# Second expert layer: scatters that add weighted rows to the output in memory, instead of a closing stage of sums

## What is computed

```
x = x + 0.5 * ffn(layernorm(x))          # mixture of experts, weights shared by both ffn calls
x = x + attn(layernorm(x))               # causal convolution, 16 blocks of 128 tokens, 8 heads
x = x + 0.5 * ffn(layernorm(x))

ffn(h):   probs = softmax(h @ router_w.T)        # 8 experts
          vals, idx = top_k(probs, 2); vals = vals / vals.sum(-1)
          out = sum over the two experts e of a token:
                vals_e * (silu(h @ gate_e.T) * (h @ up_e.T)) @ down_e.T      # hidden width 176
```

## Time and profile before

| | |
|---|---|
| median of 3 runs | 756.17 us |
| profiled execution: its own time | 758.16 us |
| profiled execution: span | 756.4 us |
| mean granted TensorE clock | 0.954 of full speed |
| PE busy | 664.9 us, 88% |
| DVE busy | 520.7 us, 69% |
| ACT busy | 491.3 us, 65% |
| POOL busy | 372.7 us, 49% |

### The profile page before, as it was taken

How to read it: one execution, slowest core, us unless ns; L and a number is a source line. 1 busy time by engine, 2 the same in 40 slices (tenths; PEclk the granted TensorE clock), 3 DMA queues, 4 the chain that set the end, 5 groups by cost and what they waited for, 6 DMA issues and landing times. The chain is left out here.

```text
span 756.4 us, 18879 instructions
## 1 busy us (share of the span) xinstructions
PE 664.9 (88%) x5168; PEld 590.6 (78%) x5169; DVE 520.7 (69%) x1829; ACT 491.3 (65%) x1702; POOL 372.7 (49%) x418
## 2 busy tenths in 40 slices
PE   3999799999996699999898989978778999999854
PEld 3986699999993577878787878767557899999743
DVE  6588466666666467787878777858657677777653
ACT  5775566666664278887877868768444566666633
POOL 4200544444424546657787877554545444444500
PEclk9999899999999789999999999999879999999968
DMA  9930345444442211111222221110224543443289
GB/s 307 304 128 10 106 141 151 143 126 133 129 111 83 77 36 36 50 42 52 77 64 64 71 72 60 33 58 22 88 89 122 160 134 120 130 127 125 71 315 351
DMA packets 60424, 85.50 MB, mean 113 GB/s; under 512 B 10032, under 2 KB 46387, under 8 KB 60340
## 3 DMA queue, kind: packets, MB, share of 16 engines
q1 hardware_dynamic: 47332, 49.73, 21.2%
q0 software_dynamic: 13008, 34.69, 14.6%
HBM read 45.77 MB, written 37.44 MB: 110 GB/s over the span
## 5 line engine op out<-in xcount | busy, mean ns | idle before, releaser
L1811 PE MATMUL CC<-w_hi,turned_parts 128*128 x568 | 175.5, 351 | 3.6 <-issue 3.6
L725 POOL DMA_INDIRECT shared<-h_rows,tok_i x71 | 70.2, 988 | 116.4 <-issue 58.9
L1811 PEld LDWEIGHTS CC<-w_hi,turned_parts 128*128 128x128 f32 x568 | 105.4, 193 | 4.4 <-issue 4.3
L742 POOL DMA_INDIRECT y_rows<-shared,y_dest x71 | 70.0, 986 | 76.0 <-DVE y_dest L1349 57.8
L818 ACT ACTIVATE shared<-CC 128x176 f32<-128x176 f32 x142 | 45.2, 319 | 76.1 <-PE CC L1811 70.1
L1811 PE MATMUL CC<-w_lo,turned_parts 128*128 x284 | 93.3, 328 | 0.0
L934 ACT ACTIVATE pr<-SS,nmax 128x128 f32<-128x128 f32 x256 | 90.5, 401 | 0.5 <-DVE nmax L1542 0.5
L758 POOL TENSOR_TENSOR pr<-pr,prec 128x1024 f32<-128x1024 f32 x31 | 58.9, 1901 | 51.4 <-DVE prec L1572 50.2
L789 POOL DMA_INDIRECT h_regions<-h_store,dest x64 | 65.4, 1022 | 34.9 <-DVE dest L1436 18.4
L1330 DVE TENSOR_TENSOR shared<-shared,CC 128x176 f32<-128x176 f32 x142 | 48.0, 338 | 49.4 <-ACT shared L818 28.0
L766 POOL DMA_INDIRECT yg<-y_rows,slot_i x64 | 62.9, 983 | 34.5 <-DMA y_rows<-shared 15.5
(11 more groups left out here) (376 smaller groups left out, 2100.3 us busy)
## 6 DMA issues: line engine op xcount, KB each, us to landing
yg<-h_regions SPq DMA_DIRECT2D x71, 129.0 KB
y_rows<-shared SPq DMA_DIRECT2D x71, 128.0 KB
w_lo<-y_rows SPq DMA_DIRECT2D x9, 512.0 KB, 8.0
x_sb<-in_x_dram SPq DMA_DIRECT2D x8, 512.0 KB, 8.3
out_dram<-x_sb SPq DMA_DIRECT2D x16, 256.0 KB, 6.2
w_hi<-y_rows SPq DMA_DIRECT2D x7, 512.0 KB, 11.8
w_lo<-in_gupT_dram SPq DMA_DIRECT2D x2, 1408.0 KB, 11.1
shared<-tile_oh SPq DMA_DIRECT2D x32, 64.0 KB
```

The source lines that it names most:

```text
L725: pool.indirect_dma_start(out=rows[:, s % RING, 0:D], out_offset=None, in_=h_dram[:, :], in_offset=bass.IndirectOffsetOnAxis(ap=tok_i[:, s ...
L742: pool.indirect_dma_start(out=y_dram[0:TOPK * TOKENS, :], out_offset=bass.IndirectOffsetOnAxis(ap=y_dest[:, s:s + 1], axis=0), in_=y_sb[:, ...
L1811: i = pe.matmul(CC[:, 512 * (u % 2):512 * (u % 2) + GU], rows_part[:, u % 2, c * P:(c + 1) * P], weights, start=(n == 1), stop=(n == 3 * DC))
```

## The change

1. `RING` becomes a module constant; rows in `h_regions` get a third extra column (`HROW = D + 3`): the difference of the token's two best logits, worked out in `pick` by one more DVE instruction (11 times).
2. Attended x is stored to the output by SP while attention runs: 12 stores of 256 KB behind the transfers of a pair, the last four in front of row loads 4 to 7 of the second layer.
3. `y_to` becomes two DVE instructions a step: the place of the token, and minus or plus a half, by whether this is the token's first expert.
4. ACT works out the share in each step: a Tanh (`turned_share`) and a Copy with scale and bias (`share_of`), each on 128 x 1, and `y_s` copies with that share as scale. The row loads wait for the Tanh too (`expd`).
5. The scatters go to the output itself, with `compute_op=ALU.add`: one row for each token. Two scatters to the same row must not be under way together, so a scatter that is the first of its expert waits until the three before it have landed. Which ones these are is known only at run time: DVE writes a table of counts (`drains`, one more compare and three more instructions for each part of the table), and POOL loads three counts from it into registers in every step and waits for each. For steps below `RING + k` the count is the constant 16, so scatters 1 to 4 always wait for the one before. Scatter 0 waits for all 16 stores (`written`).
6. The closing stage goes, with its code on all five engines.

```diff
-HROW = D + 2
+HROW = D + 3
...
+            def store_attended(g):
+                sp.wait_ge(T["res"], 2 * g + 2)
+                sp.dma_start(out_rows[:, 2 * g:2 * g + 2, :], x_view[:, 2 * g:2 * g + 2, :]).then_inc(written, 16)
...
+                        if RING <= s < RING + BEHIND:
+                            store_attended(TILES // 2 - BEHIND + s - RING)
                         if s >= RING:
                             sp.wait_ge(r["rowsT"], s + 1)
                             sp.wait_ge(r["dest"], s - RING + 1)
+                            sp.wait_ge(r["expd"], s - RING + 1)
...
+                if p >= BEHIND:
+                    store_attended(p - BEHIND)
             load_rows(1)
-            load_sums(1)
-
-            store_sums()
...
+                    if s in (RING + 1, EARLY):
+                        pool.wait_ge(T["drain_table"], 1 + s // EARLY)
+                    counts = [pool.value_load(drained_i[0:1, s, k - 1:k], min_val=16, max_val=16 * in_ring(0))
+                              if s >= RING + k else 16 for k in range(1, RING) if k <= s]
                     pool.wait_ge(r["y_sb"], s + 1 + 2)
                     pool.sem_inc(passed_pool, 1)
                     pool.wait_ge(r["dest"], s + 1)
                     pool.sem_inc(passed_pool, 1)
+                    if s == 0:
+                        pool.wait_ge(written, 16 * (TILES // 2))
+                        pool.sem_inc(passed_pool, 1)
+                    for k, count in enumerate(counts, 1):
+                        pool.wait_ge(r[f"st{(s - k) % RING}"], count)
+                        pool.sem_inc(passed_pool, 1)
                     pool.indirect_dma_start(
-                        out=y_dram[0:TOPK * TOKENS, :],
-                        out_offset=bass.IndirectOffsetOnAxis(ap=y_dest[:, s:s + 1], axis=0),
-                        in_=y_sb[:, s % RING, :], in_offset=None, bounds_check=TOPK * TOKENS - 1, oob_is_err=False
-                    ).then_inc(r[f"st{s % RING}"], 16)
+                        out=out_flat, out_offset=bass.IndirectOffsetOnAxis(ap=y_dest[:, s:s + 1], axis=0),
+                        in_=y_sb[:, s % RING, :], in_offset=None, bounds_check=TOKENS - 1, oob_is_err=False,
+                        compute_op=ALU.add).then_inc(r[f"st{s % RING}"], 16)
...
+                def turned_share(u, s):
+                    a.wait_ge(r["dest"], s + 1)
+                    a.activation(share[:, u % RING:u % RING + 1], rows_in[1][:, u % RING, D + 2:D + 3], ACT.Tanh,
+                                 scale=half_sign[:, u % RING:u % RING + 1]).then_inc(r["expd"], 1)
+
+                def share_of(u, s):
+                    of = share[:, u % RING:u % RING + 1]
+                    a.wait_ge(r["expd"], s + 1)
+                    a.activation(of, of, ACT.Copy, scale=0.25, bias=0.25).then_inc(r["scaled"], 1)
...
             experts(R[1], last_turns)
-            difference(R[1])
-            a.wait_ge(R[1]["shares"], 2)
-            last_sum()
...
+            def drains(first, end):
+
+                step(v.tensor_tensor(switched[:, first:end], expert_of[0:1, first:end],
+                                     expert_of[0:1, first - 1:end - 1], ALU.not_equal))
+                for k in range(1, RING):
+                    at = max(first, RING + k)
+                    ins = v.scalar_tensor_tensor(out=drained_i[0:1, at:end, k - 1], in0=switched[:, at:end],
+                                                 scalar=16.0, in1=steps_16[:, at - k:end - k],
+                                                 op0=ALU.mult, op1=ALU.add)
+                ins.then_inc(T["drain_table"], 1)
...
-                    v.scalar_tensor_tensor(out=y_dest[:, bass.ds(s, 1)], in0=rows_in[1][:, q, D + 1:D + 2],
-                                           scalar=expert_of[:, bass.ds(s, 1)], in1=rows_in[1][:, q, D:D + 1],
-                                           op0=ALU.not_equal, op1=ALU.add).then_inc(r["dest"], 1)
+                    v.tensor_copy(y_dest[:, bass.ds(s, 1)], rows_in[1][:, q, D:D + 1])
+                    v.tensor_scalar(half_sign[:, q:q + 1], rows_in[1][:, q, D + 1:D + 2],
+                                    expert_of[:, bass.ds(s, 1)], -0.5, ALU.not_equal, ALU.add).then_inc(r["dest"], 1)
```

More of the change, by code:

```diff
@@ L220, in macaron_kernel @@
         y_dest = sb("y_dest", [P, TABLE_TILES], I32)
+        half_sign = sb("half_sign", [P, RING])
+        share = sb("share", [P, RING])
+        oh_row = oh[0:1, :, :, :].rearrange("p i k e -> p (i k e)")
+        drained_i = oh_row[:, 0:TABLE_TILES * (RING - 1)].bitcast(I32).rearrange("p (s k) -> p s k", k=RING - 1)
+        steps_16 = oh_row[:, 256:256 + TABLE_TILES]
+        switched = oh_row[:, 384:384 + TABLE_TILES]
         best = sb("best", [P, TILES, E])
@@ L330, in macaron_kernel @@
         for L in range(2):
-            for n in ("shares", "expd", "weights_at", "g0", "g1", "g2", "g3", "rowsT", "rowsT_hi", "rowsT_lo", "gu", "silu",
+            for n in ("shares", "expd", "scaled", "weights_at", "g0", "g1", "g2", "g3", "rowsT", "rowsT_hi", "rowsT_lo", "gu", "silu",
                       "hid", "hidT", "hidT_hi", "hidT_lo",
                       "y", "y_sb", "st0", "st1", "st2", "st3", "dest"):
-                if n not in (("dest",), ("weights_at",))[L]:
+                if n not in (("dest", "scaled"), ("weights_at",))[L]:
                     R[L][n] = sem(f"r{L}_{n}")
@@ L396, in low_acc @@
             return (A, B)[at % 2][0:rows_of, 0:width]
[L398 to L418, removed]
         def in_ring(u):
@@ L466, in turns @@
                 turn(i)
-        BY_ACT = [t for t in range(TILES) if t % 8 in (2, 4, 7)]
         LOADED = 8
@@ L598, in load_rows @@
                             sp.wait_ge(r["dest"], s - RING + 1)
+                            sp.wait_ge(r["expd"], s - RING + 1)
                         sp.dma_start(rows_in[L][:, s % RING, :], h_regions[bass.ds(at, P), :]
                                      ).then_inc(r[f"g{s % RING}"], 16)
[L602 to L609, removed]
-                    sp.wait_ge(final, sum(t not in BY_ACT for t in range(2 * g + 2)))
-                    after(sp, final_act, sum(t in BY_ACT for t in range(2 * g + 2)))
-                    sp.dma_start(out_rows[:, 2 * g:2 * g + 2, :], x_view[:, 2 * g:2 * g + 2, :]).then_inc(written, 16)
-                sp.wait_ge(written, 16 * (TILES // 2))
+            def store_attended(g):
+                sp.wait_ge(T["res"], 2 * g + 2)
+                sp.dma_start(out_rows[:, 2 * g:2 * g + 2, :], x_view[:, 2 * g:2 * g + 2, :]).then_inc(written, 16)
             def store_y(L):
@@ L834, in y_s @@
                     a.wait_ge(r["y"], s + 1 + 2)
-                    after(a, r[f"st{u % RING}"], 16 * round_)
-                    a.activation(y_sb[:, u % RING, :], SS[:, 512 * (u % 2):512 * (u % 2) + D], ACT.Copy
-                                 ).then_inc(r["y_sb"], 1)
+                    y = SS[:, 512 * (u % 2):512 * (u % 2) + D]
+                    if between:
+                        a.wait_ge(r["scaled"], s + 1)
+                        after(a, r[f"st{u % RING}"], 16 * round_)
+                        a.activation(y_sb[:, u % RING, :], y, ACT.Copy, scale=share[:, u % RING:u % RING + 1]
+                                     ).then_inc(r["y_sb"], 1)
+                    else:
+                        after(a, r[f"st{u % RING}"], 16 * round_)
+                        a.activation(y_sb[:, u % RING, :], y, ACT.Copy).then_inc(r["y_sb"], 1)
+                def turned_share(u, s):
[6 more added lines that the diff above has]
+                    a.activation(of, of, ACT.Copy, scale=0.25, bias=0.25).then_inc(r["scaled"], 1)
                 rows_high(0, 0)
@@ L851, in step @@
                         silu_s(u % 2, s)
+                        if between:
+                            turned_share(u, s)
                     if is_tile(s - 1):
                         hid_high(u - 1, s - 1)
+                        if between:
+                            share_of(u - 1, s - 1)
                     if is_tile(s - 2):
@@ L1031, in first_norm @@
                         attention_weights()
-            def last_sum():
-                for n, t in enumerate(BY_ACT + [None]):
-                    if t is not None:
-                        a.wait_ge(*y_in(t // 2))
-                        for k in range(TOPK):
-                            part = slice(k * D, (k + 1) * D)
-                            ins = a.activation(scaled_pair(t)[:, part], y_pairs(t // 2)[:, t % 2, part], ACT.Copy, scale=wts[:, k, t:t + 1])
-                        ins.then_inc(scaled, 1)
-                    if n > 0:
-                        b = BY_ACT[n - 1]
-                        a.wait_ge(summed, n)
-                        a.activation(x_tile(b), (A, B)[(n - 1) % 2][:, 0:D], ACT.Copy).then_inc(final_act, 1)
             def difference(r):
```

62 lines of the change are left out of this document (16 added, 46 removed).

## The result

The changed kernel takes **809.15 us** (median of 4 runs, 807.88 to 811.7), the kernel before 756.09 us beside it (4 runs): a ratio of **1.071**, 95% interval 1.068 to 1.074. It is 53 us slower. The forecast was 792 us with a range of 722 to 812 us, slower being the likeliest: right in sign, 17 us short in size. The likeliest case's own range, 780 to 809, ends just at the measured time.

The account below looks back on a forecast made before the run. PE was taken to bound steady steps, DMA bytes the closing stage. Scatter 5 at 590, plus 48.0 us (12 changes), 151.1 (53 others), landing 3.0 and end 0.3: 792.4 us span, 36 more than before; 792 us forecast, range 722 to 812.

Parts of the forecast that it names:

- likeliest case: Whole kernel: POOL's cycle of 2.6 to 3.2 us makes it slower, 780 to 809 us; chance 0.54.
- What bounds, and what goes: Second layer and end: PE full at 2.0 us a step; the 36.5 us closing stage goes but for some 0.3 us.
- POOL's queue decides: Plain steps from 5 on: three register loads at 0.527 us lengthen POOL's cycle to 2.85 us, beyond PE's 2.0 us.
- break-even: POOL's queue: the whole change gains nothing at a cycle of 2.17 us, a load of 0.30 us for one register.
- The cheap bound: POOL's queue: a load of 0.06 us for one register gives a cycle of 1.45 us, hidden behind PE.
- Landings at changes: Scatters that change expert, 13 counted: landing 3.0 us plus 0.97 us to the next start, 4.0 us between scatters.
- The start: Scatters 0 to 5: scatter 0 at 569, the next four 4.0 us apart, scatter 5 at 590; PE hardly feels it.
- The sum: Scatter 5 to the end: 12 changes and 53 other distances, landing and end give a 792.4 us span, 792 us median.
- What costs nothing: ACT's Tanh and share, DVE's extra instruction, stores and row loads: hidden or little; DVE in attention 0 to 2 us.
- Cheap loads: Rival on POOL's queue: loads below 0.24 us hide on plain steps, kernel ends near 725 us; chance 0.26.
- Slow adding: Rival on the scatters: adding makes a landing take 8 us while loads are small, 807 us; chance 0.05.
- PE's clock: Rival on PE: its clock falls with the waiting, up to 20 us on top; no chance of its own.

Follow-up runs that it names:

- start_free: Changed kernel without register loads, waiting for landings only at the 13 known steps that change expert, not in scatters 1 to 4: 738.38 us, 1.0005 of the kernel before.
- apart_plain: Changed kernel without register loads, landing waits or adding, scattering to y_dram at two rows a token (expert rows missing from output): 0.9655 of the kernel before.
- loads_by_eight: Changed kernel with the counts of eight steps (24 registers) brought by one load from step 8 on, same three waits: 1.0188 of the kernel before.
- three_back: Changed kernel without register loads, each scatter waiting for the landing three steps before it, a constant: 713.64 us, 0.9667 of the kernel before.
- after_again: The changed kernel itself, unaltered, run again on another chip: 794.48 us, 1.0749 of the kernel before.
- loads_alone: Changed kernel keeping three loads and waits a step, but with no changes in the table, scattering to y_dram (expert rows missing): 1.0219 of the kernel before.
- before_again: The kernel before itself, unaltered, run again for its trace on another chip: 738.68 us in its one execution.

## Why the prediction was right, and where it was short

**What bounds, and what goes.** Right. From the last scatter's landing the old closing stage was 36.5 us, and all of it went. But "0.3 us until the queues end" failed: 5.6 us pass from the landing to the end, nearly all of it POOL's drain. The trace of before had it in a row, 9.304 us at 720.2, hidden under the closing stage. I had not asked what that stage itself was hiding. The term of 3.3 us for landing and end measured 8.4: +5.1 us.

**POOL's queue decides.** The step was right in place and nearly in size: cycle 2.72 us in the mean where 2.85 was forecast, -7.1 us over 53 steps. Its parts were not right. I had 0.97 + 0.3 for waits and issue and 3 x 0.527 for the loads; in the plain step of the chain it is 1.0 for waits and issue together and 3 x 0.54, 2.62 us. And the 0.54 is not one load: the load is 0.285 us, and the bounds of `value_load` bring the other half. The step "if it is the trip and not the count, one takes as long as eight. I take the second" failed, and that 0.527 came out so near 0.54 is luck. The test that I named, "their median (I say 0.53 us, and 0.3 decides)", would have called the loads cheap at 0.285. What can be held against a break-even is only all that a load brings with it, which a reader of the trace has to add up by line. The cheap bound had a second gap: 1.45 us a step counts the scatter at the plain 0.98 us, but one that adds takes POOL 1.56 us, and with the loads gone POOL's cycle is 1.86. The eight registers at 0.527 us on SP's queue were a row of the right kind for the wrong reason.

The Trainium skill (DMA: Bandwidth & Descriptors, Latency and other measured facts) gives such a load a floor of about 600 ns. This trace doesn't agree: one register took 0.285 us. That unrolling amortizes a load, as the page has it, agrees in kind: one load for eight steps can't be told from none (1.0188 and 1.0183).

**Landings at changes.** The count of 13 was right, the size not: 4.95 us in place of 4.0, +11.4 us for the twelve. The step that failed is the landing of 3.0 us, "nearer the plain one, because a scatter's packets are a small part of it". Ahead of changes it is 3.5 to 4.5 us in the chain (3.66 at 652.64, 4.54 at 602.17), 3.9 in the mean, and about 1.05 us of waits and issue follow it. Two things were in it. The 2.13 us that I started from were a scatter of filler, whose rows are skipped: filler that adds lands in 2.66 us (the scatter at 795.13), a plain scatter with rows in 2.48 in the mean ahead of changes (2.2 to 2.6, once 3.6). And adding rows takes 1.4 us more than writing them. I had bounded the landing at 4.3 and chosen too near the low end. An adding scatter goes as three times as many packets and holds each engine 1.07 us and not 0.31; that this is why it lands later is likely, but no run separates it from the adding itself. The Trainium skill (Collectives: The Full Stack, The bandwidth ceiling) speaks of two source reads in place of one, of which I made 0.3 us more; measured it is 0.76 us more of each engine. The direction agrees, and for the size two reads in place of one fall short of this case.

**The start.** Scatter 0 at 569, as forecast (569.00). Scatter 5 at 594.33 for 590, +4.3 us: the four scatters behind scatter 0 came 4.8 to 5.3 us apart. That PE hardly feels it is beside the point. After step 5 POOL leads, and start_free shows that its delay goes to the end in full, also with POOL's cycle at 1.86 us, under PE's 2.0.

**The sum.** 792.4 + 4.3 + 11.4 - 7.1 + 5.1 = 806.1 us, the measured span. Three terms too low, one too high; that the total still lay inside 722 to 812 us, at the very edge of the likeliest case, owes something to the one too high and to a range that was drawn wide enough for both signs.

**What costs nothing.** Right: Tanh was 0.302 us and not 0.204, the copy with share 0.473 us, DVE's second instruction 0.204 us, and apart_plain shows all of them and the stores hidden under PE's 2.0 us. From 540 us on ACT loads one function table, of 1.283 us, as before; the Tanh changes none.

**The rivals.** Cheap loads, about 725: not only its condition failed. With the loads made cheap (loads_by_eight) the kernel is still slower than before, 1.0188, or some 770 us by the result's 756: the landings at changes and at the start alone keep it from gaining. Near 0.966 x 756 = 730 us, as in three_back and apart_plain, it ends only when these waits go as well. Slow adding: the landing was longer than mine, but at 3.5 to 4.5 us far from 8. PE's clock: granted 0.93 in 620 to 780 us, with PE idle a fourth of the time. The plain steps don't feel it: their median is 2.65 us in after_again with a clock of 0.88 in 600 to 690 us, and 2.64 us in loads_alone with 1.00 there.

## What to carry to other kernels

A queue's cycle is the sum of everything in it, waits and register work too, and it binds long before the engine's busy share says so: POOL was 51% busy and set every step. So put loads of registers together, many steps at a time, and count the instructions that bounds on a value bring. Before a stage is removed, look for what it covers, up to the last drain. And a wait that guards against a conflict should be as wide as the conflict: here 17 waits for the landing just before cost 0.052, 38 us, on this input, while the eleven real conflicts were three steps back and cost nothing to wait for.

## What the runs showed of the hardware

- An indirect scatter that adds 128 rows of 1 KB takes POOL 1.56 us in place of 0.98, goes as 141 packets in place of 47, holds each engine 1.07 us in place of 0.31, and lands 3.5 to 4.5 us after its start ahead of changes, in place of 2.2 to 2.6 in most; with filler alone 2.7 us in place of 2.1.
- A register load on POOL's queue took 0.285 us for one register, 0.99 for three, 1.73 for 24 (medians); a fused operation on three registers 0.046 us, that of one `value_load` with bounds 0.147.
- POOL's drain at the end took 9.30 us in the four traces in which the scatters of the second layer are plain, 5.05 us in the nine with adding ones, whatever else differed. Why was not looked into.
- The same kernel took 756 us on the chip of the result and 737 to 739 us on the three chips of the experiments; the granted clock in 250 to 300 us was 0.90 in the trace of the first and 1.00 in that of before_again. What makes the difference is open.
